# Query rows moved into their stacks by DMA, and the memory read-out scaled on ScalarE, in a fused attention and LoRA kernel

## What is computed

```
q = x @ Wq.T ; k = x @ Wk.T ; v = x @ Wv.T            # q: 4 query groups x 8 heads x 16; k, v: 8 heads x 16
scores = einsum('bsqhd,bthd->bqhst', qh, kh) * scale   # scale = 1/4
a_dot  = einsum('bqhst,bthd->bsqhd', softmax(scores), vh)
sigma_q = elu(q.reshape(b, s, 4, 128))
a_mem  = sigma_q @ memory / (sigma_q @ memory_norm)
w = sigmoid(memory_weight)
out = a_dot * (1 - w) + a_mem * w
```

## Times and profile before

| | us |
|---|---|
| median of 3 runs | 5798.87 |
| lowest, highest | 5791.17, 5803.34 |
| profiled execution, time | 5802.16 |
| profiled execution, span | 5800.4 |
| PE busy in the span | 5047.0 (87%) |
| DVE busy | 3607.8 (62%) |
| ACT busy | 2482.5 (43%) |
| mean granted TensorE clock | 0.921 of 2.4 GHz |

### The profile page before, as it was taken

The page is one execution under the profiler, slowest core; times in us unless marked ns, Lnnn a source line. Parts: engine busy times, 40 slices in busy tenths (PEclk is TensorE's granted clock), DMA queues, the critical chain, the costliest instruction groups (busy, mean ns, idle before and its releaser), DMA issues.

```text
span 5800.4 us, 156843 instructions
## 1 busy us (share of the span) xinstructions
PE 5047.0 (87%) x62928; PEld 3609.5 (62%) x62928; DVE 3607.8 (62%) x7842; ACT 2482.5 (43%) x4660; POOL 692.7 (12%) x917
## 2 busy tenths in 40 slices
PE   4899989999999975988988888988988988989888
PEld 3777777777777763565565465465565565565555
DVE  3566656666666653675665665665665665756756
ACT  2333433333333322544544644634634634535535
POOL 0000000000000001111111111121121021121121
PEclk8899989999999987999999999989999989989999
DMA  1222222222222211000000000000000000000000
GB/s 55 64 55 62 65 62 54 54 62 66 61 54 62 69 43 55 2 16 16 1 16 16 1 15 16 2 15 16 1 15 16 1 15 16 1 15 16 1 15 9
DMA packets 352744, 173.97 MB, mean 30 GB/s; under 512 B 300032, under 2 KB 300800, under 8 KB 351264
## 3 DMA queue, kind: packets, MB, share of 16 engines
q1 hardware_dynamic: 343056, 146.25, 9.5%
q10 hardware_dynamic: 8976, 17.30, 1.0%
HBM read 94.79 MB, written 67.63 MB: 28 GB/s over the span
## 4 chain that ended last, share of the span: by engine, by line
issue 30%; PE 20%; DVE 7%; POOL 3%; ACT 1%; DMA 0%; DVEq 0%; POOLq 0%; SPq 0%; ACTq 0%
PE row_psum L40 5%; PE row_psum L42 5%; PE row_psum L41 5%; DVE smax L1775 3%; POOL xs L1231 2%; PE row_psum L1360 1%; PE row_psum L1497 1%; DVE stats L1601 1%; POOL rstd L1203 1%; PE row_psum L1464 1%; PE row_psum L1465 1%; PE row_psum L1479 1%; DVE xr_lo L1630 1%; DVE xs L1704 1%; DVE probs L1612 0%
## 5 line engine op out<-in xcount | busy, mean ns | idle before, releaser
L1775 DVE TENSOR_REDUCE smax<-row_psum 128x1 f32<-128x512 f32 x2048 | 1278.9, 682 | 314.6 <-PE row_psum L1497 313.6
L1329 ACT ACTIVATE probs<-row_psum 128x512 f32<-128x512 f32 x2048 | 1111.1, 602 | 513.8 <-PE row_psum L1510 409.3
L1497 PE MATMUL row_psum<-k_stack,q_stack 128*128 128x512 f32 x2048 | 876.0, 438 | 28.1 <-DVE smax L1775 24.4
L1510 PE MATMUL row_psum<-q_stack,k_stack 128*128 128x512 f32 x2048 | 840.6, 424 | 25.7 <-ACT probs L1329 13.7
L1497 PEld LDWEIGHTS row_psum<-k_stack,q_stack 128*128 128x128 f32 x2048 | 394.7, 193 | 467.6 <-DVE smax L1775 394.5
L1522 PE MATMUL row_psum<-probs,v_aug 128*32 128x512 f32 x4096 | 538.9, 604 | 9.2 <-ACT av_sb L1342 9.2
L1510 PEld LDWEIGHTS row_psum<-q_stack,k_stack 128*128 128x128 f32 x2048 | 383.3, 192 | 256.3 <-ACT probs L1329 195.3
L40 PE MATMUL row_psum<-wf_hi,xr_hi 128*128 128x320 f32 (+1 forms) x1024 | 327.3, 320 | 14.0 <-DVE xr_lo L1630 13.1
L875 DVE TENSOR_TENSOR lane_t<-lane_t,lane_p 128x30 f32<-128x30 f32 (+14 forms) x960 | 318.3, 332 | 33.0
L872 DVE TENSOR_TENSOR lane_p<-lane_t 128x30 f32<-128x30 f32 (+14 forms) x960 | 316.1, 329 | 25.5
L1360 PE MATMUL row_psum<-ident,probs 128*128 128x128 f32 x784 | 169.2, 373 | 179.2 <-DVE probs L1612 179.2
(11 more groups left out here) (207 smaller groups left out, 10060.2 us busy)
## 6 DMA issues: line engine op xcount, KB each, us to landing
xs<-x SPq DMA_DIRECT2D x17, 1024.0 KB, 5.6
x_sp<-in_x ACTq DMA_DIRECT2D x33, 512.0 KB, 4.4
tri_dram<-tri SPq DMA_DIRECT2D x256, 64.0 KB, 2.4
lane_t<-tri_dram SPq DMA_DIRECT2D x32, 512.0 KB, 3.5
inv_dram<-lane_t SPq DMA_DIRECT2D x32, 512.0 KB, 2.6
inv_b<-inv_dram SPq DMA_DIRECT2D x256, 64.0 KB, 2.4
x_res<-in_x SPq DMA_DIRECT2D x32, 512.0 KB, 3.7
x<-x_res SPq DMA_DIRECT2D x32, 512.0 KB, 2.8
```

Source lines behind the costliest of these rows:

```text
L1329: act.activation(probs[:, h % PROBS, tt, :], ps[:, m % STACK_BANKS, :], ACT.Exp, scale=float(DH) ** -0.5).then_inc(exp_ready, 1)
L1497: pe.matmul(ps[:, STACK_BANKS + m % MAX_BANKS, :], q_stack[:, qt, P * st:P * st + P], k_stack[:, kv, :], start=True, stop=True).then_inc(m ...
L1510: pe.matmul(ps[:, m % STACK_BANKS, :], k_stack[:, kv, P * tt:P * tt + P], q_stack[:, qt, :], start=True, stop=True).then_inc(score_mm, 1)
L1775: dve.tensor_reduce(smax[:, g, st:st + 1], ps[:, STACK_BANKS + (NT * g + st) % MAX_BANKS, :], AX.X, ALU.max).then_inc(max_ready, 1)
```

## The change

Heads in the stacks now lie 48 rows apart without gaps (rows 0 to 47 and 48 to 95), and the two shift rows are rows 96 and 97. The maxima contract over 96 rows, the scores over 98. Only the four tiles of query group 0 are still made by `pick_q` and `q_pair`. The twelve tiles of groups 1 to 3 are filled by 24 DMAs a batch that SP issues ahead of the shift rows: each moves 16 partitions x 3 tiles x 512 elements (96 KB) from `q_hi` or `q_lo` to the stacks. PE waits for all of them (`q_moved`) ahead of the first maximum of step 8. DVE keeps the reciprocal and its multiplication by w, and ACT does the multiplication of the memory products by it: four instructions of 128 columns a tile, with the reciprocal as a per-partition scale. The table `head_rows` is loaded by six DMAs in place of one, and `sel` is rounded by three ACT instructions in place of one, to re-order their rows.

```diff
+HR = 3 * DH
+MAX_ROWS, SCORE_ROWS = 2 * HR, 2 * HR + 2
+MOVED = 3 * NKV
...
-            sp.dma_start(head_rows[:, :, :].rearrange("p h c -> p (h c)"), head_rows_in).then_inc(c_in, 16)
+            rows = head_rows[:, :, :].rearrange("p h c -> p (h c)")
+            for to, of, size in ((0, 0, HR), (HR, 64, HR), (2 * HR, HR, 1), (2 * HR + 1, 64 + HR, 1),
+                                 (2 * HR + 2, HR + 1, 15), (2 * HR + 17, 64 + HR + 1, 15)):
+                sp.dma_start(rows[to:to + size, :], head_rows_in[of:of + size, :]).then_inc(c_in, 16)
...
                     sp.dma_start(xs[:, 1 - par, :, :], x2_rows[ahead]).then_inc(x_loaded[1 - par], 16)
+                    for part, split, done in ((0, q_hi, qhi_ready), (2, q_hi, qhi_ready), (1, q_lo, qlo_ready)):
+                        sp.wait_ge(done, at(b, NQ, NQ))
+                        for h in range(NKV):
+                            r0 = HR * (h % 2) + DH * part
+                            sp.dma_start(q_stack[r0:r0 + DH, HP + h // 2:NQ * HP:HP, :].bitcast(F32),
+                                         split[DH * h:DH * h + DH, 1:NQ, :].bitcast(F32)).then_inc(q_moved, 16)
                     for quad in range(QUADS):
                         sp.wait_ge(shift_ready, at(b, QUADS, quad + 1))
                         for i in range(4):
                             n, h = head(quad, i)
-                            r0 = 64 * (h % 2) + 3 * DH
+                            r0 = MAX_ROWS + h % 2
...
+                    def memory(t):
+                        act.wait_ge(rc_ready, at(b, NT, t + 1))
+                        for n in range(NQ):
+                            last = act.activation(a_mem[:, t, DKV * n:DKV * n + DKV],
+                                                  ps[:, 6 + n // 2, (DKV + 1) * (n % 2):(DKV + 1) * (n % 2) + DKV],
+                                                  ACT.Copy, scale=mem_rc[:, t, n:n + 1])
+                        last.then_inc(amem_ready, 1)
...
-                            first = 1 + 2 * g + j
-                            if g < SCORE_LAG and first > 2:
-                                q_pair(first)
-                                if first == 2 * SCORE_LAG:
-                                    q_pair(first + 1)
+                            if (g, j) == (1, 0):
+                                q_pair(HP - 1)
...
+                            if j == 0 and 0 <= g - MEM_LAG < NT:
+                                memory(g - MEM_LAG)
...
-                        pe.matmul(ps[:, STACK_BANKS + m % MAX_BANKS, :], q_stack[:, qt, P * st:P * st + P], k_stack[:, kv, :],
+                        pe.matmul(ps[:, STACK_BANKS + m % MAX_BANKS, :], q_stack[0:MAX_ROWS, qt, P * st:P * st + P], k_stack[0:MAX_ROWS, kv, :],
                                   start=True, stop=True).then_inc(max_mm, 1)
...
-                            first = 1 + 2 * g + j
-                            if g < SCORE_LAG:
-                                pick_q(first)
-                                if first == 2 * SCORE_LAG:
-                                    pick_q(first + 1)
+                            if 1 + 2 * g + j < HP:
+                                pick_q(1 + 2 * g + j)
                             if g < NH:
-                                if g % 2 == 0 and j == 0:
-                                    pe.wait_ge(qstack_ready, at(b, NQ * HP, pair(g)[0] + 1))
+                                if g % 2 == 0 and g < NKV and j == 0:
+                                    pe.wait_ge(qstack_ready, at(b, HP, pair(g)[0] + 1))
+                                if g == NKV and j == 0:
+                                    pe.wait_ge(q_moved, at(b, 16 * MOVED, 16 * MOVED))
                                 maximum(g, 2 * j)
...
-                        mark(dve.tensor_scalar(rc, rc, mem_w[:, 0:1], None, ALU.mult))
-                        dve.wait_ge(dve_own, own[0])
-                        for c in range(2):
-                            last = dve.tensor_tensor(a_mem[:, t, 2 * DKV * c:2 * DKV * c + 2 * DKV].rearrange("p (n e) -> p n e", n=2),
-                                                     pv[:, c, :, 0:DKV],
-                                                     rc[:, c, :].rearrange("p (n o) -> p n o", o=1).to_broadcast([P, 2, DKV]), ALU.mult)
-                        last.then_inc(amem_ready, 1)
+                        dve.tensor_scalar(rc, rc, mem_w[:, 0:1], None, ALU.mult).then_inc(rc_ready, 1)
```

More of the change, by code:

```diff
@@ L1123, in token_layers @@
         vtok_mm = sem("vtok_mm"); v_ready = sem("row_v_ready")
-        ksel_mm = sem("ksel_mm"); keven_ready = sem("keven_ready"); kodd_ready = sem("kodd_ready"); qsel_mm = sem("qsel_mm"); qstack_ready = sem("qstack_ready")
+        q_moved = sem("q_moved"); rc_ready = sem("rc_ready"); ksel_mm = sem("ksel_mm"); keven_ready = sem("keven_ready"); kodd_ready = sem("kodd_ready"); qsel_mm = sem("qsel_mm"); qstack_ready = sem("qstack_ready")
         mem_mm = sem("mem_mm"); amem_ready = sem("amem_ready"); amem_added = sem("amem_added")
@@ L1195, in _ @@
             pool.wait_ge(pool_consts, 3)
-            pool.wait_ge(c_in, 112)
+            pool.wait_ge(c_in, 192)
             def inverse_std(b, f):
@@ L1241, in _ @@
                 d2 = dst[:, :] if n == 1 else dst[:, :, :].rearrange("p k n -> p (k n)")
-                act.activation(d2, stage[:, 0:size], ACT.Copy).then_inc(w_hi_done, 1)
-            act.wait_ge(c_in, 112)
+                if dst is not sel:
+                    act.activation(d2, stage[:, 0:size], ACT.Copy).then_inc(w_hi_done, 1)
+                    continue
+                drawn = stage[:, 0:size].rearrange("p (k e r) -> p k e r", e=2, r=64)
+                for e in range(2):
+                    act.activation(sel[:, :, HR * e:HR * e + HR], drawn[:, :, e, 0:HR], ACT.Copy)
+                act.activation(sel[:, :, 2 * HR:P].rearrange("p k (e r) -> p k e r", e=2), drawn[:, :, :, HR:64], ACT.Copy).then_inc(w_hi_done, 1)
+            act.wait_ge(c_in, 192)
             act.activation(mem_w[:, :], mem_w[:, :], ACT.Tanh, scale=0.5).then_inc(mem_tanh, 1)
@@ L1292, in q_pair @@
                     def q_pair(m):
-                        act.wait_ge(qsel_mm, at(b, NQ * HP, m + 1))
+                        act.wait_ge(qsel_mm, at(b, HP, m + 1))
                         act.activation(q_stack[:, m, :], ps[:, (HP + m) % STACK_BANKS, :], ACT.Copy).then_inc(qstack_ready, 1)
@@ L1351, in _ @@
             pe.wait_ge(w_hi_done, 5)
-            pe.wait_ge(c_in, 112)
+            pe.wait_ge(c_in, 192)
             pe.wait_ge(pool_consts, 3)
@@ L1430, in stack_bank @@
                         elif before >= HP:
-                            pe.wait_ge(qstack_ready, at(b, NQ * HP, before - HP + 1))
+                            pe.wait_ge(qstack_ready, at(b, HP, before - HP + 1))
                         return tile % STACK_BANKS
@@ L1503, in score @@
                         if h == 0 and tt == 0:
-                            pe.wait_ge(qstack_ready, at(b, NQ * HP, NQ * HP))
+                            pe.wait_ge(qstack_ready, at(b, HP, HP))
                         if h % 4 == 0 and tt == 0:
@@ L1509, in score @@
                             pe.wait_ge(exp_ready, at(b, NT * NH, m - STACK_BANKS + 1))
-                        pe.matmul(ps[:, m % STACK_BANKS, :], k_stack[:, kv, P * tt:P * tt + P], q_stack[:, qt, :],
+                        pe.matmul(ps[:, m % STACK_BANKS, :], k_stack[0:SCORE_ROWS, kv, P * tt:P * tt + P], q_stack[0:SCORE_ROWS, qt, :],
                                   start=True, stop=True).then_inc(score_mm, 1)
@@ L1589, in _ @@
             dve.wait_ge(dve_consts, 2)
-            dve.wait_ge(c_in, 112)
+            dve.wait_ge(c_in, 192)
             dve.wait_ge(pool_consts, 3)
```

## The result

The change made the kernel slower by 1.0%: 5860.4 us median against 5801.1 us for the kernel before on the same chip, ratio 1.0098 [1.0078, 1.0117]. The forecast was 5889 us. The profiled execution took 5861.55 us (span 5859.7), 59.4 us more than the 5802.16 of before.

A forecast was written before the change was run, and what follows sets the result against it. PE bounds the body; in the lead-in, the chain through DVE to the transpose of the second four heads' maxima. 16 x (4.5 queue + 1.0 clock) + 2.5 preamble = 90 us gave 5892 profiled, 5889 median; range 5785 to 5985.

The forecast's parts named there:

- the signs named in advance: After-trace: first-score shift wait 4 to 7 us a batch, moves at 105 to 130 GB/s, DVE idle in step 7.
- The price of a move: Lead-in DMAs: 24 moves at 114 GB/s take 20.7 us, ending at 3661.8.
- What queues behind them: SP's queue: shift rows land behind all moves; first score at 3662.4, not 3657.44, transpose 4.5 us later.
- Rival 1: Lead-in: moves hidden, costing only their issue, 0.5 to 0.59 us each; about 5802 us; chance 0.24.
- the case with 0.58: Lead-in: moves hold up the first score; own range 5833 to 5970 us; chance 0.58.
- 0.17 us a step is lost: Lead-in memory steps: ACT's read-out replaces DVE's in the chain, 3.7 us a step against 3.53.
- 1.0 us for the dozen instructions: PE after idling in the lead-in: instructions at half clock before recovery cost 1.0 us a batch, bounds 0 and 1.5.
- rival 3: Thin lead-in loses the clock: memory step about 1.1 us longer, 3.5 us a batch, 5857 us; chance 0.06.
- Picks, copies and layout at nothing: Lead-in: removed picks nearly all covered by DVE's pace, ACT copies worth nothing, 96 or 98 rows cost nothing.
- The preamble's 2.5 us: Ahead of the first x: five more small DMAs at 0.5 us issue each, 2.5 us once.
- the stretch behind the first score: Lead-in, first score at 3662.4 to transpose at 3670.5: 0.7 us to memory tile 2, then 7.4 us.
- Rival 4: Moves: rate goes with partitions touched, 2 us a move, batch 27 us more, 6230 us; chance 0.02.

The follow-up runs named there:

- Moves alone: Changed kernel with the memory read-out back on DVE as in the kernel before: 5821.4 us, 1.0051.
- Moves alone with the shift rows first: Changed kernel with the read-out on DVE and the first four heads' shift rows issued ahead of the q_lo moves: 5794.6 us, 1.0001.
- the read-out alone: Kernel before with only the memory read-out moved to ACT, all 16 picks kept: 5853.1 us, 1.0107.
- Filler: Twelve unread matmul pairs a batch where the picks stood: on the changed kernel 5852.9 us, 1.0102; on moves alone 5825.3 us, 1.0042.
- after with order and shift rows first: Changed kernel with memory products issued a step earlier and first shift rows ahead of the q_lo moves: 5848.1 us, 1.0092.
- order and read-out: Kernel before with memory products issued a step earlier and the read-out on ACT, all picks kept: 5789.8 us, 0.9994.
- layout with preamble: Kernel before with only the 48-row layout and its preamble, all picks, read-out on DVE, no moves: 5807.2 us, 1.0010.
- Layout with the read-out and all picks: Kernel before with the 48-row layout and the read-out on ACT, all 16 picks, no moves: 5911.3 us, 1.0196.

## Why the prediction was right, and where not

**Direction and place.** Slower was right (0.69), and so was the chain: DVE's pace, memory tiles, and the transpose that ends the lead-in. It comes 3.34 us later where the forecast had 5.5. The launch loses 59 us where the forecast had 90. Of the signs named in advance, ACT's time for a tile (1.14 us), the release of the memory product by ACT and DVE's idle time in step 7 held. The pace of the moves (150 and 153 GB/s, not 105 to 130) and PE's wait for the shift rows did not:

```profile
L1535 PE MATMUL row_psum<-q_stack,k_stack 98*128 98x512 f32 x2048 | 856.2, 432 | 46.2 <-ACT probs L1352 30.6 <-DMA q_stack<-shift 9.6
```

That is 9.6 us in the whole launch, 0.42 in the batch shown, and not 4 to 7 a batch.

**The price of a move: wrong.** "I take 114 GB/s" made data the bound. The moves leave SP every 0.595 us in the median, which is 98,304 B / 0.595 us = 165 GB/s; the issue of a shift row, of 2 KB, takes 0.589 in the median in before, so this looks like the bare issue. Issuing all 24 takes 15.5 us, and the windows show 150 and 153 GB/s. The DMA share of 0.90 suggests that the data is close behind as a bound., chosen as nearest in kind, are of transfers with one end in DRAM. With 3.0 us to landing, the last lands 15.5 - 0.6 + 3.0 = 17.9 us behind the first issue, not 21.9. The Trainium skill, "SBUF — State Buffer", section "Door 1: The DMA port swizzle", gives 104 GB/s for partitions 0 to 15; this trace does not agree for a train of moves. Moves of neighbouring heads touch other partitions and overlap (3.0 us to landing, 0.6 apart), and no run here times one alone, so what a single transfer would show is left open.

**What queues behind them: right in kind, too large.** The shift rows did stand behind the moves, and the first score waited. It came 1.50 us later (22.47 against 20.97), not 5.0. Rival 1 has it at most 1.0 us later (3658.4 against 3657.44), so the truth lies between it and the forecast, and nearer to it: on the moves that rival, at 0.24, was closer than the case with 0.58. Moves alone cost 0.51% (1.0051 [1.0034, 1.0068]), and with the shift rows first nothing of it is left (1.0001). That the queue serves in ring order, as "DMA: Bandwidth & Descriptors", section "Queues, rings and completion order", of the Trainium skill states for one engine, fits these runs; what they show is only SP's order of issue.

**The memory read-out on ACT: the term that was mis-sized.** Its instructions were forecast well: 1.15 us for four, measured 1.14; the transpose waits for ACT, as said. But "0.17 us a step is lost" counts the duration of the read-out and not its wait at the head of ACT's queue: 2.3 to 3.5 us of idle ACT ahead of each. In step 7 exponentials stand behind it, a score behind those, and the memory product behind the score. From the first score to the end of the lead-in 8.52 us passed before and 10.36 after, where the forecast had 8.1 and clock. Alone the read-out costs 1.07%, as much as the whole change with its 0.98%: there the stack copies, which the moves take off ACT, stand behind it too, and PE waits for them 2.9 us a batch. The effects do not add: 1.07 and 0.51 make 0.98.

**The clock: seen, and worth less than charged.** "1.0 us for the dozen instructions" and rival 3 (3.5 us a batch) both charge it. The half clock lasted much longer than I had it, 17.5 us a batch. Filler that brings the full clock back changes neither after (1.0098 and 1.0102) nor moves alone (1.0051 and 1.0042) by more than the intervals; in the lead-in of after it gives back 0.7 us net of its own work. Moves alone with the shift rows first has 11.1 us of half clock at 1.0001: there PE had the slack. Rival 3's mechanism, a slower memory step, shows itself where the ring leads through PE: in after with order and shift rows first, whose lead-in is 2.7 us a batch longer than that of order and read-out.

**Picks, copies and layout at nothing: right.** Moves alone, well ordered, is 1.0001; layout with preamble is 1.0010, at most 1.0021. Neither gains anything, since DVE sets the pace. The preamble's 2.5 us is near what the trace shows: the load of the first x is issued 5.19 us behind that of `mem_aug`, and 3.32 before, 1.9 us more.

**How the errors met.** The term for the queue was 3.5 us a batch too large (5.0 against 1.5), and the stretch behind the first score 2.3 too small (8.1 against 10.36). What the clock costs lies inside those 10.36 us, so its own term of 1.0 goes: 5.5 - 3.5 - 1.0 + 2.3 = 3.3. The time fell inside the range because errors of both signs met, and that is luck: about half of the loss (0.98 less 0.51) came with the read-out, which I had charged with 0.17 us a step. Rival 4's sum is wrong: its moves take 27 us a batch more than those of the forecast, so its time is near 6320, not 6230; at a chance of 0.02 that changes nothing.

**Open.** Layout with the read-out and all picks is 0.9% above the read-out alone, though the layout alone is 0.1%. Its lead-in is 1.0 us longer, with 8.1 us of half clock against 5.3, and its body 1.5 us longer, with 5.4 against 1.5. Over all kernels the body is shortest where it has no half clock (95.1 us in order and read-out) and longest here (97.1). So a lower clock goes with the loss, and why it fell more in this kernel is not known. Nor has an experiment settled the whole change with both cures: filler on that kernel would tell whether the half clock is all that is left.

## What to carry to other kernels

Before moving work from a full engine to one with room, look at what stands behind it in the new engine's queue, and price the wait for its input at the head of that queue, not only its duration. The same holds for DMA issue: small urgent transfers go ahead of bulk ones that are needed later. A lost clock matters where TensorE is on the chain: here it cost nothing measurable while VectorE set the pace, while in the ring through ScalarE a memory step took 4.8 us at half clock and 4.1 at full (in the traces; no experiment isolates it). So find the chain before filling gaps; and a product that a chain passes through is worth issuing a step early.

## What the hardware showed that I had not expected

Moves of 96 KB between 16 and 16 partitions of SBUF, one behind another on one queue, run at 0.595 us each (median of 256), 150 and 153 GB/s over 4 us each, well above the 105 to 130 of the earlier trace rows. A batch's lead-in ran at half clock for 11 us at no measurable cost (1.0001 [0.9991, 1.0010]), while in the ring through ACT a memory step took 4.79 us at half clock, against 4.14 at full in order and read-out.
